# Moving four small DMA reads per attention group from the SyncE queue to the ScalarE queue, and two residual loads behind them

## The reference, cut to what matters

```
def attention(q, k, v, mask):                      # 16 heads of width 32
    scores = einsum('bhqd,bhkd->bhqk', q, k) / sqrt(32)
    scores = scores * mask - 10000.0 * (1.0 - mask)
    probs  = softmax(scores, axis=-1)
    return einsum('bhqk,bhkd->bhqd', probs, v)

x = x + attention(q, k, v of layernorm(x)) @ w_ao + b_ao                 # self-attention
x = x + attention(q of layernorm(x); k, v of ctx_2048) @ w_co + b_co     # cross-attention
x = x + gelu(layernorm(x) @ w1 + b1) @ w2 + b2                           # perceptron
x = batchnorm(w_w @ ((theta(x) phi(ctx) / 512) g(ctx)) + w_b) + x        # non-local block
```

## Time and profile before

| | |
|---|---|
| median of three runs | 2017.9 us |
| the profiled execution | 2019.01 us, its span 2017.2 us |
| turns 1 to 14 | some 73 us each, from about 135 to 1160 us of the span |
| VectorE busy over the span | 73% |
| ScalarE busy over the span | 58% |
| mean granted TensorE clock | 0.998 of full speed |

### The profile page before, as it was taken

How to read it: one execution, slowest core, us unless ns; L and a number is a source line. 1 busy time by engine, 2 the same in 40 slices (tenths; PEclk the granted TensorE clock), 3 DMA queues, 4 the chain that set the end, 5 groups by cost and what they waited for, 6 DMA issues and landing times. The chain is left out here.

```text
span 2017.2 us, 41550 instructions
## 1 busy us (share of the span) xinstructions
PE 1980.1 (98%) x13632; PEld 1571.8 (78%) x13632; DVE 1470.2 (73%) x3868; ACT 1160.5 (58%) x3251; POOL 546.7 (27%) x556
## 2 busy tenths in 40 slices
PE   9999999999999999999999998999999999999998
PEld 9877777777777777777777776888888888888887
DVE  7799989998998998998899989564444343435333
ACT  4388788887888888888887888521212111212111
POOL 1012212222234343333334342054032231313000
PEclk9999999999999999999999999999999999999999
DMA  8446676576678877767777744531212213121201
GB/s 284 161 94 129 151 172 141 132 166 143 132 190 183 185 185 167 167 171 180 152 173 179 162 109 118 171 101 41 78 38 72 68 44 81 47 62 50 62 24 48
DMA packets 681720, 252.67 MB, mean 125 GB/s; under 512 B 533312, under 2 KB 626112, under 8 KB 681536
## 3 DMA queue, kind: packets, MB, share of 16 engines
q1 hardware_dynamic: 563264, 235.69, 45.3%
q10 hardware_dynamic: 118272, 14.69, 4.7%
HBM read 167.41 MB, written 82.84 MB: 124 GB/s over the span
## 5 line engine op out<-in xcount | busy, mean ns | idle before, releaser
L1331 ACT ACTIVATE A_p<-A_p,A_nmax 128x256 f32<-128x256 f32 x1024 | 507.2, 501 | 3.7 <-DVE A_res L1614 1.7
L1646 DVE CUSTOM_DVE_ANT_0 A_p<-A_p,A_ma 128x256 f32<-128x256 f32 x1024 | 374.6, 420 | 4.6
L1636 DVE TENSOR_TENSOR A_p<-A_sc,A_mk 128x1024 f32<-128x1024 f32 x256 | 312.2, 1220 | 52.7 <-PE A_tp L1093 52.0
L842 POOL TENSOR_TENSOR A_ct_l<-A_cx,A_ct_h 128x256 fp32r<-128x256 f32 x122 | 114.1, 935 | 679.6 <-DVE A_nmax L1646 666.1
L1348 ACT ACTIVATE A_pt<-A_tp 128x512 f32<-128x512 f32 x396 | 218.1, 587 | 49.1 <-PE A_tp L1093 47.6
L1093 PEld LDWEIGHTS A_tp<-A_ident,A_p 128*128 128x128 f32 x1584 | 179.9, 141 | 73.0 <-ACT A_p L1331 36.6
L1093 PE MATMUL A_tp<-A_ident,A_p 128*128 128x128 f32 x1584 | 223.6, 278 | 2.9 <-ACT A_pt L1348 2.1
L1485 ACT ACTIVATE A_mk<-A_tp,A_cols 128x512 f32<-128x512 f32 x62 | 42.7, 689 | 269.0 <-PE A_tp L68 269.0
L1331 ACT ACTIVATION_READ_ACCUMULATOR A_p<-A_p,A_nmax 128x1 f32 x1024 | 197.5, 193 | 0.0
L1485 ACT ACTIVATE A_ma<-A_tp,A_cols 128x512 f32<-128x512 f32 x62 | 42.8, 690 | 243.0 <-PE A_tp L68 243.0
L66 PE MATMUL A_banks<-A_xt_h,A_w_h 128*128 128x512 f32 x384 | 162.1, 422 | 8.8 <-DVE A_res L1614 8.3
(11 more groups left out here) (248 smaller groups left out, 4997.1 us busy)
## 6 DMA issues: line engine op xcount, KB each, us to landing
exponentials<-A_ln_shift SPq DMA_DIRECT2D x464, 64.0 KB, 2.4
A_pt<-exponentials SPq DMA_DIRECT2D x116, 256.0 KB, 4.2
A_x<-x SPq DMA_DIRECT2D x96, 256.0 KB, 3.9
A_res<-x SPq DMA_DIRECT2D x64, 256.0 KB, 3.2
A_rt<-inverses SPq DMA_DIRECT2D x512, 32.0 KB, 2.2
x<-A_res SPq DMA_DIRECT2D x64, 256.0 KB, 4.7
turned<-A_x ACTq DMA_DIRECT2D x224, 64.0 KB, 2.8
A_e<-ctx_t SPq DMA_DIRECT2D x16, 512.0 KB, 4.1
```

Source lines behind the costliest of these rows:

```text
L842: pool.tensor_tensor(ct_l[:, f, part], cx[:, :], f32(ct_h[:, f, part]), ALU.subtract).then_inc(c_lo, 1)
L1331: act.activation(p[:, g % 2, j, t, :], p[:, g % 2, j, t, :], ACT.Exp, scale=-1.0, bias=nmax[:, g % 2, j, t:t + 1], accum_out=rsum[:, g % 2 ...
L1636: dve.tensor_tensor(p[:, g % 2, heads, :, :].rearrange("p j t s -> p j (t s)"), sc[:, heads, :], m, ALU.mult)\
L1646: dve.tensor_tensor_reduce(out=a_, in0=a_, in1=ma[:, b, t, :], scale=-1.0, scalar=BIG, op0=ALU.add, op1=ALU.min, accum_out=nmax[:, g % 2, ...
```

## The change

Two things are changed. The four reads of the reciprocals are issued by ScalarE instead of SyncE, one behind each of the exponentials 3, 4, 5 and 6 of the slot; the first of them has the wait for the landing of the store in front. This is so in the slots in which there is both an own group and a present one, but not in slots 6 and 7 of turn 0, in slots 4 and 5 of the turns 1 to 14, or in the slots behind turn 15, where SyncE goes on to issue them. And the two residual loads of slot 6 stand behind `store_exponentials` and the place of `load_inverses`.

```diff
+        def beside_exponentials(k, h):
+            return k < NU and exists(k, h, 0) and exists(k, h, -1) and not late(k, h) and not (by_blocks(k) and h in (4, 5))
...
             def slot(r, k, h, a_, b_, own, pv):
...
                     store_inverses(r, h)
-                    if h == 6 and 0 < k < NU:
-                        for t in range(2):
-                            load_res(k - 1, r - 1, t + 2)
                 if exists(k, h, 0) and moved(group(r, h, 0)[0]):
                     store_exponentials(r, h)
-                if own:
+                if own and not beside_exponentials(k, h):
                     load_inverses(r, h)
+                if h == 6 and 0 < k < NU:
+                    for t in range(2):
+                        load_res(k - 1, r - 1, t + 2)
...
                 if by_blocks(k) and h in (4, 5):
                     write_block(k, r, 2 * h - 8 + n // 4, n % 4)
+                if beside_exponentials(k, h) and 3 <= n < 3 + HPG:
+                    load_inverse(r, h, n - 3)
+
+            def load_inverse(r, h, j):
+                grp, _, g = group(r, h, -1)
+                if j == 0:
+                    wait_apart(act, st_i, (grp + 1) * DMA, cx_ok, grp)
+                act.dma_start(*inverses_of(j, g)).then_inc(ld_i, DMA)
```

More of the change, by code:

```diff
@@ L431, in raw_pair, with inverses_of @@
             return e[:, n, :, :] if k < NB else f32(xt_l[:, :, 2 * n * P:(2 * n + 2) * P])
+        def inverses_of(j, g):
+            blocks = inv_dram[g % 2].rearrange("(n c) s -> n (c s)", c=32).rearrange("(a n) s -> a n s", a=1)
+            return (rt[j * HD:(j + 1) * HD, :].rearrange("p (n s) -> p n s", n=P // 32),
+                    blocks[:, :, j * TPB * 32:(j + 1) * TPB * 32].broadcast_to([HD, P // 32, TPB * 32]))
+        def beside_exponentials(k, h):
+            return k < NU and exists(k, h, 0) and exists(k, h, -1) and not late(k, h) and not (by_blocks(k) and h in (4, 5))
         def late(k, h):
@@ L548, in load_inverses @@
                 wait_apart(sp, st_i, (grp + 1) * DMA, cx_ok, grp)
-                blocks = inv_dram[g % 2].rearrange("(n c) s -> n (c s)", c=32).rearrange("(a n) s -> a n s", a=1)
                 for j in range(HPG):
[L551 to L554, removed]
+                    sp.dma_start(*inverses_of(j, g)).then_inc(ld_i, DMA)
             def store_exponentials(r, h):
```

## The result

The changed kernel took 2043.9 us as the median of four runs (2037.5 to 2045.3), the kernel before 2018.9 as the median of four, one more than ahead of the prediction (2016.6 to 2021.8). The ratio is 1.0118, with a 95% interval of 1.0101 to 1.0136: 24 us slower. I had forecast 10 us slower. The direction and the stretch in which the time would lie were right, the size was less than half of what came. The profiled execution of the changed kernel is the fastest of its four (2037.5 us, span 2035.3), so the two traces lie 18 us apart, and not 24.

A forecast was written before the change was run, and what follows sets the result against it. The prediction took TensorE, busy 98% of the span, as the bound, with waits its only gain. Its terms, -16 + 17 + 3 + 0 + 1 + 3 + 2 = +10 us, gave 2028 us by the median, range 2008 to 2047.

The forecast's parts named there:

- Part 1: Slot 7's scaling and slot 0's residual add: reads released at the store's landing come in time, TensorE's waits go; -16 us.
- Part 2: Slot 6: ScalarE's wait for the store delays its packed work, so TensorE waits for v in slot 7; +17 us.
- delays d: Landing of the reciprocals' store minus start of exponential 3; in slot 6 forecast at 25.1 us summed over 14 turns.
- Part 3: Slot 0: ScalarE's wait delays k_h, k_l and the product needing their bank; +3 us, ends 0 and +10.
- Part 4: Slots 7, 1, 2, 3: stores land early, 0; slot 0's reads beside four 256 KB loads, +1 us, ends 0 and +14.
- Parts 5 and 6: Late landings in turns 7, 8, 15 and one slot of turn 2, +3 us; issue time of 372 reads, +2 us.
- not drained: Rival: the small store lands in slots 0 and 1 as late as now, all moved slots pay; 2051 us, chance 0.13.

## Why the prediction was wrong, step by step

**Part 1, -16, is the step that failed.** It took the reads' landing time from rows in which little stood beside them, "about 2 us to land", and moved only their issue. They were issued 1.2 us earlier against the landing of the store, as forecast, and landed later: 6.7 us after it on the mean in slot 6, where it had been 5.4. The scaling in slot 7 waits 1.4 us instead of 1.0, and the stall at slot 0 stayed at 0.8 us a turn (it fell to 0.3 in turns 3 to 6 and stayed at 1.0 in turns 9 to 14). Booked -16, got -1.7 in slot 0 and nothing in slot 7. With the bytes cut the last read of slot 6 lands in 2.6 us on the mean and the stall goes, so the mechanism of the stall was right, and only the landing time was not.

**Part 2, +17, held as a mechanism, and its size in part by luck.** TensorE waits for v in each of the 14 turns, 0.9 us in the turn shown, as worked out for turn 9, and 13.1 us in all. The sum of the delays d came out at 22.7 us, where 25.1 were forecast. Slot 7 grew by 16.6 us, but this holds late reads too (2.8 us of waits for the scaling), and the 2.6 us of turn 7, where TensorE's clock fell for a while behind its waits. Moving the reads behind exponential 5 took the wait for v away, which shows that it was the place of the wait. And the term can't simply be added to part 1: ScalarE's wait by itself cost 8 us in the whole kernel, since part of the old stall goes under in it.

**Part 3, +3, with its ends 0 and +10, came to nothing.** The delay d of slot 0 shrank as argued, and further: the store lands 2.9 us after its issue instead of 4.0, and d is -0.5 to 1.0 us where I left it at 0.3 to 1.4. The product it would delay is the first of slot 1, and there TensorE waits for k_l only twice, 0.5 us together.

**Part 4, 0 and +1.** That the stores of slots 7 and 1 find a drained queue was right: 2.2 and 2.0 us instead of 4.1 and 4.2. The +1 for the reads of slot 0 beside four loads was mis-sized. The last of them took 4.6 us instead of 2.4, the scaling in slot 1 came late by 0.4 us on the mean, with it k_l, and slot 2 lost 7.0 us, of which 2.4 only moved there from slot 1; 1.0 us a turn was my end for it. Here I had a rule beside the row: by the Trainium skill, DMA: Bandwidth & Descriptors (Queues, rings and completion order), an engine takes turns between rings. The runs don't refute that, but a ring of their own did not keep these reads from being slow beside 1 MB of another's, so my step from the rule to a term of 0 was wrong. The same page of the Trainium skill, in its section "Issuing engines are not separate DMA queues", says that DMAs run on the same 16 engines whoever started them, and that a second issuer only saves the sequencer's issue time. That agrees with the 4.3 to 6.3 us above, and I should have weighed it instead.

**Parts 5 and 6** are small in the trace: turns 7 and 8 carry some 2 us of the loss, turn 15 next to nothing. Of 372 issues on ScalarE the median was 0.39 us, and one took over 1 us where I had counted with 7 to 15.

**The sum.** Without the gain of part 1, my own terms give 10 + 16 = 26 us; 24 were measured, and the traces lie 18 apart. That the first two agree is in part luck: parts 3, 5 and 6 were booked at 8 us and show little more than 2 in the slots, while slot 2 lost more than was booked for it. The rival nearest to it, "not drained", had a time of 2051 for the wrong reason: the stores were drained, and the reads were not.

**What the halves say.** I booked the residual loads at nothing, "wanted by GpSimd a slot later". That half alone costs 10 us. I looked at who wants the moved loads and not at what they then stand ahead of.

What stays open: the changed kernel's four runs lie 6 us higher in the median than the one profiled, and which slots carry these 6 us no trace shows. Reads on ScalarE without any wait and without big loads beside them weren't tried. Nor does any run tell why four small reads suffer so much. The page of the profile says that they are cut fine: with them ScalarE's queue carries 53,568 packets more than before, which is 144 for each 32 KB read. Whether fewer and larger pieces would fare better wasn't tried.

## What to carry to other kernels

A wait in a queue of DMAs is also a spacing of what stands behind it. Before a small, urgent transfer is taken off such a queue, list the bytes that will then go out in the same microseconds, and price its landing by rows in which something stands beside it. If a queue idles in a wait anyway, put there the transfers that nobody wants soon, ahead of the wait: that was worth 9 us here, where handing the wait to a packed engine cost 8.

## What the runs showed of the hardware that I had not expected

Four 32 KB reads from ScalarE's queue took 4.3 to 6.3 us to land with 1 MB requested on SyncE's queue in the same 1.5 us, 2.4 to 2.9 with that cut to a quarter or less, though the page of the profile lists the two as queues of their own (q10 and q1). And ScalarE's sequencer, when the store had landed in time, issued a read ahead of its place in the engine's work: in 68 of the 93 slots the read that stands behind exponential 3 went out before that exponential started, by 0.9 us at the median. In slot 7 of turn 13 it went out at 1098.08, and the exponential started at 1099.28:

```profile
1098.08 0.34 ACTq L1348 DMA_DIRECT2D A_rt<-inverses  x1
1098.31 0.49 ACT L1337 ACTIVATE A_p<-A_p,A_nmax 128x256 f32<-128x256 f32 x1
...
1099.28 0.50 ACT L1337 ACTIVATE A_p<-A_p,A_nmax 128x256 f32<-128x256 f32 x1
```
